# A rewritten self-attention stage in a decoder layer, its copies of transposed probabilities split between ScalarE and VectorE

## The reference, cut to what matters

```python
q = (hidden_states @ Wq).reshape(b, s, 32, 16)
kv = hidden_states @ Wkv                  # one key and one value head of 16, shared by 32 query heads
k, v = (kv[..., :16], kv[..., 16:])
scores = jnp.einsum('bqhd,bkd->bhqk', q, k) * 16 ** -0.5
scores = jnp.where(causal, scores + slopes[:, None, None] * (key_pos - query_pos), -jnp.inf)
attn = jax.nn.softmax(scores, axis=-1)
out = jnp.einsum('bhqk,bkd->bqhd', attn, v).reshape(b, s, 512)
return out @ Wo
```

## Time and profile before

| | |
|---|---|
| median of 3 runs | 1018.83 us (1015.87 to 1019.94) |
| the profiled execution: its time, its span | 1015.36 us, 1013.5 us |
| self stage, from the first instruction to the cross stage's first matmul | 0 to 234.52 us |
| cross stage and feed-forward | 234.52 to 1013.5 us |
| TensorE / VectorE / ScalarE / GpSimd busy over the span | 97% / 58% / 42% / 38% |

### The profile page before, as it was taken

The page is one execution under the profiler, slowest core; times in us unless marked ns, Lnnn a source line. Parts: engine busy times, 40 slices in busy tenths (PEclk is TensorE's granted clock), DMA queues, the critical chain, the costliest instruction groups (busy, mean ns, idle before and its releaser), DMA issues. The chain is left out here.

```text
span 1013.5 us, 15742 instructions
## 1 busy us (share of the span) xinstructions
PE 985.4 (97%) x5128; PEld 808.2 (80%) x5128; DVE 589.1 (58%) x973; ACT 429.1 (42%) x1239; POOL 382.0 (38%) x375
## 2 busy tenths in 40 slices
PE   5999999989999999999999999999999989999998
PEld 3877777877888888888888888888888768888787
DVE  3856566635776676666666767667666773343100
ACT  2777676751433533523533533533432543333100
POOL 6422222163652642652642633634623422222200
PEclk9999999989999999999999999999999999999999
DMA  6000000211120210210210200210300012122001
GB/s 202 13 11 11 11 10 10 63 52 52 32 63 11 55 50 0 72 31 0 72 31 0 72 31 0 73 30 11 82 1 0 33 32 68 67 71 74 10 32 42
DMA packets 41538, 40.17 MB, mean 40 GB/s; under 512 B 3104, under 2 KB 28832, under 8 KB 41504
## 3 DMA queue, kind: packets, MB, share of 16 engines
q1 hardware_dynamic: 41120, 38.68, 12.7%
q0 software_dynamic: 384, 1.05, 0.3%
HBM read 37.62 MB, written 2.10 MB: 39 GB/s over the span
## 5 line engine op out<-in xcount | busy, mean ns | idle before, releaser
L624 PE MATMUL bank<-cross_wo_hl,cross_outT_hl 128*128 128x512 f32 x768 | 191.7, 398 | 1.0 <-POOL cross_wo_hl L618 0.6
L624 PE MATMUL bank<-hsT_hl,cross_wqkv_hl 128*128 128x512 f32 x768 | 188.2, 394 | 0.0
L624 PEld LDWEIGHTS bank<-cross_wo_hl,cross_outT_hl 128*128 128x128 f32 x768 | 143.1, 188 | 35.5 <-POOL cross_wo_hl L618 1.6
L624 PEld LDWEIGHTS bank<-hsT_hl,cross_wqkv_hl 128*128 128x128 f32 x768 | 141.9, 188 | 29.3
L937 ACT ACTIVATE cross_scores<-cross_scores,cross_negmax 128x128 f32<-128x128 f32 x256 | 99.8, 391 | 127.1 <-DVE cross_negmax L875 127.1
L797 POOL TENSOR_TENSOR cross_qT<-rotated,rotated_other_half 128x512 f32<-128x512 f32 x64 | 82.8, 1293 | 161.9 <-DVE rotated_other_half L839 161.9
L624 PE MATMUL bank<-hsT_hl,ff_gate_upT_hl 128*128 128x512 f32 (+1 forms) x528 | 120.4, 390 | 2.7 <-DVE ff_gate_upT_hl L1139 2.7
L624 PEld LDWEIGHTS bank<-hsT_hl,ff_gate_upT_hl 128*128 128x128 f32 (+1 forms) x528 | 97.7, 185 | 25.0 <-DVE ff_gate_upT_hl L1139 3.1
L947 ACT CAST cross_outT_hl<-bank 128x512 fp32r<-128x512 f32 x64 | 37.1, 579 | 143.4 <-PE bank L624 142.5
L837 DVE TENSOR_TENSOR rotated<-bank,cosT 128x512 f32<-128x512 f32 x80 | 55.2, 690 | 71.4 <-PE bank L624 71.3
L624 PE MATMUL bank<-ctxT_hl,cross_wqkv_hl 128*128 128x512 f32 x384 | 94.3, 394 | 1.1 <-PEq L74 1.1
(11 more groups left out here) (117 smaller groups left out, 1535.6 us busy)
## 6 DMA issues: line engine op xcount, KB each, us to landing
staged_rows<-in_wq SPq DMA_DIRECT2D x32, 256.0 KB, 2.8
staged_rows<-in_wo SPq DMA_DIRECT2D x32, 256.0 KB, 2.7
staged_rows<-in_wg SPq DMA_DIRECT2D x11, 256.0 KB, 2.5
staged_rows<-in_wu SPq DMA_DIRECT2D x11, 256.0 KB, 2.6
staged_rows<-in_wd SPq DMA_DIRECT2D x11, 256.0 KB, 2.7
ctx_tok<-in_ctx SPq DMA_DIRECT2D x8, 256.0 KB, 2.6
staged_rows<-in_wk SPq DMA_DIRECT2D x8, 256.0 KB, 3.0
staged_rows<-in_wv SPq DMA_DIRECT2D x8, 256.0 KB, 3.0
```

The source lines that it names most:

```text
L624: i = nc.tensor.matmul(out, stationary[:, a], moving[:, b], start=(first and k == 0), stop=(last and k == 2))
```

## The change

The self stage is written anew; the cross and feed-forward stages are the same code. What it does:

- The layer norms of the first 4 sequences, and Q for those 4, are made before the first score (`before_attention`); the other norms and Q, KV and output products are placed in steps by a table (`steps_in`) and go through three PSUM banks (`MB`). These products are fp32r in high and low parts (`products`).
- The bias comes out of the score product: rows for slope and position stand under Q and K, and one fp32r product of 256 columns makes two heads, two of them a quad (`scores`). The stacked Q is made by 12 DMAs from SBUF to SBUF for each sequence (`stack_queries`), issued by SyncE in the order of `load_q`, 6 of the first sequence's by ScalarE.
- VectorE adds a causal mask, takes the maximum and inverts the row sums that the exponentials accumulate (`accum_out`); GpSimd scales the probabilities by them (`probs`).
- The transposed probabilities of even quads are copied out of PSUM by ScalarE, of odd quads by VectorE (`probsT` in both queues).
- The value products hold V still and stream the probabilities: 4 fp32 products of 512 columns for 4 quads, each on 32 columns of the array and 32 partitions of the output (`values`). The output needs no transposing.
- The context comes transposed from the host's layout, so its transposes are gone; its chunks are loaded and split in steps of sequences 4 and 5 (`CTX_CHUNKS`).

```diff
+            load_q(0, (0, 1))
+            load_q(1)
+            load_q(2)
+            load_q(3)
+            load_ctx(0)
+            load_ctx(1)
+            load_q(4)
+            for j in range(2, 5):
+                load_ctx(j)
+            load_q(5)
+            for j in range(5, 8):
+                load_ctx(j)
             for j in range(PIECES):
+                if j == 0:
+                    sp.wait_ge(sem["wo1_low"], QUAD)
+                if j == SLOTS:
+                    load_q(6)
+                    load_q(7)
                 load_piece(sp, m, sem, j, j % SLOTS, piece_source(io, j, 0), first=j < SLOTS)
...
+            def load_ctx(j):
+                if j >= 2:
+                    sp.wait_ge(sem["ctx_low"], j - 1)
+                sp.dma_start(ctx[:, j % 2, :], io["ctx"][j // 2][:, (j % 2) * HT:(j % 2 + 1) * HT]).then_inc(sem[f"ctx_loaded{j % 2}"], 16)
...
+CTX_CHUNKS = {(b, s): 4 * (b - 4) + s // 2 for b in (4, 5) for s in (1, 3, 5, 7)}
...
+            for b in range(SEQS):
+                for s in range(STEPS):
+                    n = STEPS * b + s
+                    dve.wait_ge(sem["scores1"], n + 1)
+                    if n >= SLOT_S:
+                        dve.wait_ge(sem["probs_transposed1"], n - SLOT_S + 1)
+                    nc.vector.tensor_tensor(S[:, n % SLOT_S], SC[n % 2][:].rearrange("p (h k) -> p h k", h=QUAD),
+                                            causal[:].unsqueeze(1).to_broadcast([P, QUAD, P]), ALU.add).then_inc(sem["biased1"], 1)
+                    dve.wait_ge(sem["biased1"], n + 1)
+                    nc.vector.tensor_reduce(negmax[:, n % SLOT_S, :], S[:, n % SLOT_S], AX.X, ALU.max, negate=True).then_inc(sem["max1"], 1)
+                    if n >= 1:
+                        dve.wait_ge(sem["exp1"], n)
+                        nc.vector.reciprocal(rinv[:, (n - 1) % SLOT_S, :], rowsum[:, (n - 1) % SLOT_S, :]).then_inc(sem["rinv1"], 1)
+                    if n >= 4 and n % 2 == 0:
+                        probsT(n - 3)
+                    for kind, i in ended_in(b, s):
+                        read_bank(kind, i)
...
+                    if n >= 3 and n % 2 == 1:
+                        probsT(n - 3)
+                    act.wait_ge(sem["max1"], n + 1)
+                    for j in range(QUAD):
+                        e = nc.scalar.activation(S[:, n % SLOT_S, j, :], S[:, n % SLOT_S, j, :], ACT.Exp, bias=negmax[:, n % SLOT_S, j:j + 1],
+                                                 accum_out=rowsum[:, n % SLOT_S, j:j + 1])
...
+                    if b == SEQS - 1 and s >= 2:
...
+                        piece_high(nc, act, m, sem, (s - 2) % SLOTS, (s - 2) // SLOTS + 1, m["wqkv_hl"][:, s - 2])
+            probsT(STEPS * SEQS - 2)
+            attnT_high(SEQS - 1)
...
+                for j in range(QUAD):
+                    e = nc.tensor.matmul(OB[32 * j:32 * j + 32, :], v[:, b, 0:32] if second else v[:, b, 16:48],
+                                         PT[:, (QUAD * w + j) % SLOT_PT], start=not second, stop=bool(second))
...
+            scores(0)
+            for b in range(SEQS):
+                for s in range(STEPS):
+                    n = STEPS * b + s
+                    if n + 1 < STEPS * SEQS:
+                        scores(n + 1)
+                    if n >= 3:
+                        transposes(n - 3)
+                    if n >= 7 and n % QUAD == 3:
+                        values(n // QUAD - 1)
+                    for kind, i, tiles in steps_in(b, s):
+                        step(kind, i, tiles)
...
+    for group, part in GROUPS_OF_ROWS:
+        queue.dma_start(qT[32 * group:32 * group + 32, b % RINGS].rearrange("p (c r) k -> p c r k", r=QUAD)[:, :, r, :].bitcast(F32),
+                        q_hl[32 * r:32 * r + 32, part, :, at:at + P].bitcast(F32)).then_inc(sem[f"q_loaded{b % RINGS}"], 16)
```

More of the change, by code:

```diff
@@ new lines, in last_of, with bank_uses, use_of, highs_before @@
+def last_of(kind):
+    return 3 if kind in ("q", "kv", "out") else 0
+def bank_uses():
+    uses = [(kind, i) for kind, i, tiles in before_attention()]
+    for b in range(SEQS + 1):
+        for s in range(STEPS):
+            uses += [(kind, i) for kind, i, tiles in steps_in(b, s) if last_of(kind) in tiles]
+    return uses
+USES = bank_uses()
+def use_of(kind, i):
+    return USES.index((kind, i))
+def highs_before(u):
+    return sum(1 for kind, i in USES[:u] if kind != "out")
+def ended_in(b, s):
+    if s == 0:
+        b, s = b - 1, STEPS
+    return [(kind, i) for kind, i, tiles in steps_in(b, s - 1) if last_of(kind) in tiles] if b >= 0 else []
@@ L174, in keys_by_head @@
[L174 to L184, removed]
@@ L375, in body @@
+            act.wait_ge(sem["wkv1_loaded"], 16)
+            nc.scalar.copy(wkv_hl[:, 0], wkv[:]).then_inc(sem["wkv1_high"], 1)
+            for c in range(HALF):
+                high("q", c)
+            act.wait_ge(sem["bank_read"], use_of("q", HALF - 1) + 1)
+            for r in (2, 3):
+                stack_queries(act, sem, qT, q_hl, 0, r)
+            high("kv", 0)
+            high("vt", 0)
+            for b in range(SEQS):
                 for s in range(STEPS):
                     n = STEPS * b + s
-                    if s == 1 and scores and since(b, 1):
-                        copy_qT(b, 1)
@@ L422, in _ @@
[L422 to L427 removed]
+                    for kind, i in ended_in(b, s):
+                        high(kind, i)
+                    if b >= 1 and s == 4:
+                        attnT_high(b - 1)
+                    if n >= 3 and n % 2 == 1:
+                        probsT(n - 3)
+                    act.wait_ge(sem["max1"], n + 1)
@@ L576, in _ @@
-            with pe.Fori(3, SEQS - 1) as b:
-                body(b)
-            for b in range(SEQS - 1, SEQS + 1):
-                body(b)
+                    if n + 1 < STEPS * SEQS:
[5 more added lines that the diff above has]
+                    for kind, i, tiles in steps_in(b, s):
+                        step(kind, i, tiles)
@@ new lines, in _, with stack_queries @@
+            for n in range(STEPS * SEQS - 3, STEPS * SEQS):
+                transposes(n)
+            values(2 * SEQS - 1)
+            step("out", SEQS - 1, (0, 1, 2, 3))
+def stack_queries(queue, sem, qT, q_hl, b, r):
+    at = (b % HALF) * P
+    for group, part in GROUPS_OF_ROWS:
+        queue.dma_start(qT[32 * group:32 * group + 32, b % RINGS].rearrange("p (c r) k -> p c r k", r=QUAD)[:, :, r, :].bitcast(F32),
+                        q_hl[32 * r:32 * r + 32, part, :, at:at + P].bitcast(F32)).then_inc(sem[f"q_loaded{b % RINGS}"], 16)
```

780 lines of the change are left out of this document (370 added, 410 removed).

## The result

The changed kernel takes 1028.95 us (median of 4 runs, 1028.35 to 1030.46), the kernel before 1017.35 in the same session: ratio 1.0114 [1.0086, 1.0143]. It is slower by 1.1%, and the interval lies above 1; I forecast 1011.8 us and faster.

The account below looks back on a forecast made before the run. TensorE's queue was taken to bound the old quads, VectorE and ScalarE the new. Start 38, loop 160, query waits 12 and end 17.5 sum to 227.5 us against 234.5, so 1011.8 us for the kernel, range 999 to 1029.

Parts of the forecast that it names:

- first mask add: Start of the self stage: norms, Q, transfers and KV evictions put VectorE's first mask add at 38 us, against 20.93 before.
- add to last exponentials, without query waits: Quad loop: VectorE's 145 us of work, 10 of waits between queues, 5 for sequence 1 and Q products; 160 us.
- end: From the last exponentials to the self stage's end: 17.5 us (14 to 20), against 14.3 before.
- The stacked queries: Starts of sequences 5 and 6: VectorE waits 7.4 and 4.5 us for late transfers priced at 0.42 us an issue; 12 together.
- The other sequences' transfers have over 8 us to spare: Query transfers outside sequences 5 and 6: they land over 8 us early, so nothing waits for them.
- Sequence 1 adds 2 us: Sequence 1 of the loop: five KV evictions on ScalarE, then two on VectorE, in line, add 2 us.
- first Q product: Start: after four norms and the weight's low parts on VectorE and GpSimd, Q begins at 15.4 us.
- value set's 2.15 us: TensorE's set of four value products: 5 slots, 2.15 us, between bounds of 0.86 and 3.44; it decides only from 2.3 on.
- Rival 2: TensorE's clock falls during the quads: half clock for a quarter of the loop costs 14 us, 1026 us; chance 10%.
- Rival 3: The stacked queries cost nothing because SyncE issues and lands them faster: 12 us less, 999.8 us; chance 12%.
- a first add past 42 us: Sign of being wrong, at the start: the first mask add comes later than 42 us, where 38 was expected.
- a clock below 0.9 in the quads: Sign of being wrong, in the loop: TensorE's granted clock under 0.9, where 1.00 was expected.

Follow-up runs that it names:

- b5: e1 with VectorE making the weight's last two low parts and GpSimd issuing three of ScalarE's six first-sequence query transfers: 1003.64 us, ratio 0.9862.
- e1: Changed kernel with SyncE's order altered so the stacked queries of sequences 5 to 7 go ahead of context chunks and weight pieces: 1006.97 us, ratio 0.9902.
- b6: e1 with the KV product of sequences 4 to 7 moved one step later: 1005.75 us, ratio 0.9882.
- e7: e1 with each score product made three times, to keep TensorE busier: 1014.87 us.
- e11: Changed kernel with queries of sequences 6 and 7 ahead of the weight pieces but behind the context chunks: 1026.13 us, ratio 1.0091.
- e10: Changed kernel with half of the query transfers of sequences 5 and 6 issued by GpSimd, SyncE's order kept: 1025.52 us, ratio 1.0092.
- e8: e1 with 128 columns of V held in each value product, so a set's four products run one after the other: 1023.63 us.
- b2: e1 with GpSimd's first weight-piece split moved into step 3 of the last sequence: 1005.25 us, ratio 0.9879.
- e3: Changed kernel with all copies of transposed probabilities on ScalarE, none on VectorE: 1028.21 us, ratio 1.0122.

## Why the prediction was wrong

| term | predicted | measured |
|---|---|---|
| first mask add | 38 | 43.65 |
| add to last exponentials, without query waits | 160 | 168.2 |
| waits for stacked queries | 12 | 19.4 |
| end | 17.5 | 15.9 |
| stage | 227.5 | 247.1 |

The stage came out 19.6 us longer than the sum: 8.2 in the loop without the query waits, 7.4 in the query waits, 5.7 in the start, and 1.6 less at the end. Each of the first two alone is more than the 7 us of gain that I had forecast.

The step that failed first is "The stacked queries": "A small transfer costs SyncE 0.42 us to issue". The mechanism, the two places and the instructions queued ahead were right, the price was not: I took it from one transfer of 2 KB from memory, and a 64 KB transfer inside SBUF costs 0.64 to 0.67 us to issue in the changed kernel. From the mask add of step 5 (144.84 us) to the one that opens sequence 5 pass 16.7 us, where I had 13.4: 5.4 to the first issue (I had 5.6), 8.0 for the twelve (5.0), 1.5 from there to the score (2.3) and 1.8 from the score to the add (0.5), since the add also waits for the transposes, and both ran at the lower clock (0.79 and 1.05 us). The price lay inside my bounds (0.37 to 0.84), I chose the near end, and it enters 12 times at each place. No run shows that a full queue makes it: three issues by themselves on ScalarE (b5) take 2.03 us, 0.68 each. The trace of before already held dearer issues of SyncE than the one that I took:

```profile
4.31 0.76 SPq L121 DMA_DIRECT2D self_wo<-in_wo  x1
5.11 0.67 SPq L122 DMA_DIRECT2D cap<-in_mask  x1
```

The same price is in the start (six issues 4.01 us, not 2.5). "The other sequences' transfers have over 8 us to spare" failed too: those of sequence 4 came 1.28 us late for VectorE. Behind the waits the queues also refill, 1.6 us in sequence 6. That the waits as a whole decide the sign is shown: e1 takes those of sequences 5 and 6 away, and the kernel is faster than before. My price of an issue alone does not decide it: with waits of 12 us instead of 19.4 the changed kernel would take some 1021.5 us (an estimate, 1028.95 less 7.4), still above 1017.35.

The second miss, and the larger one, is the loop. In "Sequence 1 adds 2 us" it added 7.4 (26.61 against 19.18). The KV product stands between a mask add and the next scores; b6 shows a part of it (1.3 us). Another 2.2 us is gone in e1, e7 and e11, whose clock in that sequence is 0.89 to 1.00 instead of 0.74; in e10, with the same code there, it takes 25.42 us at 0.87. That the clock is the cause there is argued, not shown. In all VectorE's idle time beside the query waits was 22.5 us, where I had allowed 15: 7.8 in sequence 1 and 2.2 to 3.5 in each of sequences 4 to 7, the refilling among them, where I had 1.2. The third is the first Q product, 18.65 against 15.4: b5 wins 1.7 of the 3.3 us back by taking GpSimd's two low parts away; VectorE's second and third statistics also wait for their x, until 5.67 and 8.83 us.

Right were the work of VectorE and ScalarE, the places of the two large query waits, the cross stage. The end came out shorter, since the last value set took 1.93 us and not 4.0. The value set's 2.15 us was too much (1.07), without consequence below 2.3 us. The Trainium skill (TensorE: Matmul & The Clock Gate, Part 3, Packing small matmuls) has 2.38 times for three products; here four take 1.07 us beside e8's 3.60 to 3.67, 3.4 times. Rival 2 came true in the clock (0.75 to 0.83 in late sequences) and not in its cost there (e7, b2); at the stage's end the clock costs the output products 2 us, about as I had it. Rival 3 was wrong in its condition. Of the signs of being wrong two came: a first add past 42 us, and a clock below 0.9 in the quads.

## What to carry to other kernels

Read the price of a DMA issue from a transfer of the same kind, and where none is in the trace carry both bounds through every place in which it counts. In an in-order queue, order the loads by when their reader needs them and not by when they were written down: chunks for a later stage stood ahead of queries that the next step waited for, and that order turned a gain of 1% into a loss of 1%. The split of the copies between two engines could not be judged while both waited for something else (e3): take such a wait away first, then measure the split.

## What the runs showed of the hardware

- Issuing a 64 KB transfer from SBUF to SBUF takes 0.64 to 0.70 us on SyncE (12 in 7.67 and 8.04, 24 in 16.54, 6 in 4.17), 0.67 to 0.68 on ScalarE (6 in 4.01, 3 in 2.03), and 0.55 to 0.60 on GpSimd (3 in 1.65 to 1.81, e10); a 256 KB piece from memory takes 0.54 on SyncE (4 in 2.16), and 1.04 (4 in 4.14) in e10, while GpSimd was issuing.
- Four fp32 products on 32 columns each take 1.07 us at full clock and 1.93 at the lower level, against 3.60 with all 128 columns.
- The granted clock was 0.82 over the whole new loop, between 0.68 and 1.00 by sequence; in the loop before it was 1.00. A lower clock did not always make a sequence longer: sequence 0 takes 21.46 us at 0.68, and 21.48 at 0.94 (e7).
